# A fused attention and mixture-of-experts kernel: the written-out order of the steps of its middle and last batches is replaced by another

## What is computed

```python
q, k, v = split(x @ W_qkv);  q, k = rope(q, k)
w = softmax(q @ k.T / sqrt(16) + causal_mask)
x = layernorm(x + (w @ v) @ W_o)
gate = top_2(softmax(x @ Wg + bg)), normalized
x = layernorm(x + sum_e gate_e * (x @ We_e.T + be_e))
```

## Time and profile before

| | |
|---|---|
| median of three runs | 3236.32 us (3235.18 to 3238.13) |
| span of the profiled execution | 3236.3 us |
| TensorE (PE) busy | 3109.0 us, 96% |
| VectorE (DVE) busy | 2677.5 us, 83% |
| ScalarE (ACT) busy | 1884.1 us, 58% |
| GpSimd (POOL) busy | 1200.8 us, 37% |
| TensorE clock granted, mean | 0.983 of full speed |

### The profile page before, as it was taken

The page is one execution under the profiler, slowest core; times in us unless marked ns, Lnnn a source line. Parts: engine busy times, 40 slices in busy tenths (PEclk is TensorE's granted clock), DMA queues, the critical chain, the costliest instruction groups (busy, mean ns, idle before and its releaser), DMA issues.

```text
span 3236.3 us, 58547 instructions
## 1 busy us (share of the span) xinstructions
PE 3109.0 (96%) x18752; PEld 1711.5 (53%) x18752; DVE 2677.5 (83%) x8452; ACT 1884.1 (58%) x4253; POOL 1200.8 (37%) x1414
## 2 busy tenths in 40 slices
...
DMA packets 174819, 210.95 MB, mean 65 GB/s; under 512 B 26008, under 2 KB 124592, under 8 KB 174256
## 3 DMA queue, kind: packets, MB, share of 16 engines
q1 hardware_dynamic: 173056, 202.98, 36.1%
...
## 4 chain that ended last, share of the span: by engine, by line
PE 84%; DVE 8%; issue 3%; ACT 2%; DMA 1%; POOL 1%; SPq 0%; ACTq 0%; DVEq 0%; POOLq 0%
PE bank L1052 23%; PE attend L1147 15%; PE scores L1125 14%; PE bank L1109 14%; PE bank L1089 6%; PE bank L1171 3%; PE bank L1098 3%; DVE bank L902 2%; PE bank L1155 1%; PE bank L1077 1%; PE bank L1162 1%; PE bank L1179 1%; DVE maxima L905 1%; PE bank L1203 1%; PE bank L1188 1%
## 5 line engine op out<-in xcount | busy, mean ns | idle before, releaser
L778 ACT ACTIVATE weights<-scores 128x512 f32<-128x512 f32 (+3 forms) x3072 | 1333.1, 494 | 926.0 <-PE scores L1125 913.5
L902 DVE CUSTOM_DVE_ANT_0 bank<-bank,far_q 128x128 f32<-128x128 f32 (+3 forms) x2048 | 962.9, 512 | 202.4 <-PE bank L1109 186.0
L1125 PE MATMUL scores<-q_stack,k_stack 99*128 99x512 bf16 (+3 forms) x3072 | 822.1, 329 | 16.6 <-DMA q_stack<-lowrows 7.3
L1109 PE MATMUL bank<-k_stack,q_stack 96*128 96x512 bf16 (+3 forms) x3072 | 799.5, 332 | 26.3 <-DMA k_stack<-parts_scratch 8.3
L692 POOL TENSOR_SCALAR_AFFINE_SELECT weights<-weights 128x512 f32<-128x512 f32 x512 | 325.5, 637 | 1253.5 <-ACT weights L778 1253.3
L905 DVE TENSOR_REDUCE maxima<-bank 128x1 f32<-128x512 f32 x1024 | 644.1, 682 | 72.6 <-PE bank L1109 72.4
L1147 PE MATMUL attend<-weights,values 128*32 128x512 f32 (+3 forms) x6144 | 583.0, 494 | 1.4 <-POOL weights L692 1.0
L1125 PEld LDWEIGHTS scores<-q_stack,k_stack 99*128 99x128 bf16 x3072 | 279.8, 97 | 417.8 <-ACT weights L778 151.6
L1109 PEld LDWEIGHTS bank<-k_stack,q_stack 96*128 96x128 bf16 x3072 | 276.7, 98 | 398.5 <-issue 166.4
L1052 PE MATMUL bank<-wexp_hi,zT_hi 128*128 128x512 f32 x1024 | 382.2, 454 | 11.1 <-DVE lowrows L922 11.1
L1026 DVE SCALAR_TENSOR_TENSOR z<-bank,picked,z 128x256 f32<-128x256 f32 x512 | 247.6, 484 | 114.6 <-PE bank L1052 105.6
...
## 6 DMA issues: line engine op xcount, KB each, us to landing
parts_scratch<-parts SPq DMA_DIRECT2D x128, 384.0 KB, 2.5
q_stack<-parts_scratch SPq DMA_DIRECT2D x384, 128.0 KB, 7.2
k_stack<-parts_scratch SPq DMA_DIRECT2D x384, 128.0 KB, 7.8
...
q_stack<-lowrows SPq DMA_DIRECT2D x192, 8.0 KB, 2.4
...
```

The costliest lines, as they stand in the source:

```text
L778: act.activation(weights[:, n % NW, hh, c0:CH], st[(QUAD * n + hh) % NS][:, c0:CH], ACT.Exp, scale=DH ** -0.5).then_inc(S["weights_ready"], 1)
L902: dve.tensor_tensor_reduce(out=b[:, 0:w], in0=b[:, 0:w], in1=far_q[:, CH - w:CH], scale=1.0, scalar=-SENTINEL, op0=ALU.add, op1=ALU.max, a ...
L1109: pe.matmul(b[:, 0:w], q_stack[0:ROWS, n, hh, qt * P:(qt + 1) * P], k_stack[0:ROWS, n, hh, kc * CH:kc * CH + w], start=True, stop=True).th ...
L1125: pe.matmul(st[(QUAD * n + hh) % NS][:, c0:CH], k_stack[0:MROWS, s, hh, kb * P:(kb + 1) * P], q_stack[0:MROWS, s, hh, qc * CH + c0:(qc + 1 ...
```

## The change

Two tables of text are replaced, MIDDLE and LAST. Both lists hold the same steps as before, 607 in MIDDLE and 462 in LAST; only their order differs. EARLY, FIRST, POST and all functions stay. LAST is again MIDDLE without the steps that serve a next batch. The core of the diff in MIDDLE (the rows of the table begin with the item of ST that leads them; LAST has the same places):

```diff
-XL.0 XL.1 XT.0 XL.2 XT.1 XL.3 B.0.0.0 B.0.0.1 MC.3
-ST.0.0 ST.0.1 B.0.0.2 B.0.0.3 B.0.1.0 B.0.1.1 ST.0.2 ST.0.3 MASK.0 B.0.1.2 PV.46 PV.47 YE.3.1 B.0.1.3
-ST.1.0 B.0.2.0 ST.1.1 B.0.2.1 ST.1.2 B.0.2.2 ST.1.3 MASK.1
-ST.2.0 MT.3 B.0.2.3 XR.0 XR.1 ST.2.1 YT.3.1 ST.2.2 ST.2.3 MASK.2 PV.0 VCOPY.3 PV.1 XT.2
...
-ST.4.0 B.0.3.2 B.0.3.3 LOAD.0 B.0.4.0 ST.4.1 QK.0.0 ROPE.0.0 B.0.4.1 B.0.4.2 B.0.4.3 ST.4.2 ST.4.3 WO.0.0 PV.2
-  PV.3 YE.0.0
...
-ST.10.0 ST.10.1 GL.0 ST.10.2 N1A.1 ST.10.3 B.0.11.0 MASK.10 B.0.11.1 B.0.11.2 B.0.11.3 PV.8 PV.9 B.1.0.0 YT.0.0
...
-ST.18.0 ST.18.1 B.1.4.3 B.1.5.0 B.1.5.1 B.1.5.2 ST.18.2 ST.18.3 B.1.5.3 PV.16 PV.17 LOAD.1 B.1.6.0 B.1.6.1
...
-ST.23.0 B.1.11.1 ST.23.1 ST.23.2 B.1.11.2 B.1.11.3 B.2.0.0 ST.23.3 MASK.23
...
-ST.37.0 B.3.0.3 B.3.1.0 B.3.1.1 B.3.1.2 ST.37.1 ST.37.2 YT.2.1 MOE.1.2.0 CAST.1.3.1 B.3.1.3 ST.37.3 MASK.37
-  LOAD.3 B.3.2.0
-ST.38.0 ST.38.1 MOE.1.2.1 ST.38.2 ST.38.3 B.3.2.1 B.3.2.2 MT.2 MASK.38 PV.36 PV.37
...
-ST.46.0 N2A.1 ST.46.1 B.3.9.2 VP.1 B.3.9.3 B.3.10.0 B.3.10.1 ST.46.2 ST.46.3 MASK.46 PV.44 PV.45
-ST.47.0 B.3.10.2 B.3.10.3 B.3.11.0 VP.2 B.3.11.1 ST.47.1 B.3.11.2 VP.3 ST.47.2 ST.47.3 MASK.47 B.3.11.3
+B.0.0.0 XL.0
+ST.0.0 ST.0.1 B.0.0.1 ST.0.2 B.0.0.2 PV.46 PV.47 B.0.0.3 B.0.1.0 B.0.1.1 LOAD.0 YE.3.1 MC.3 ST.0.3 B.0.1.2 XT.0
+ST.1.0 B.0.1.3 ST.1.1 B.0.2.0 XL.1 XL.2 ST.1.2 YT.3.1 XT.1 B.0.2.1 MT.3 MASK.0 ST.1.3 B.0.2.2 MASK.1
+ST.2.0 ST.2.1 QK.0.0 ST.2.2 B.0.2.3 B.1.0.0 ROPE.0.0 PV.0 PV.1 B.1.0.1 ST.2.3 B.0.3.0 B.1.0.2 XT.2
...
+ST.14.0 MOE.0.0.1 B.1.5.0 CAST.0.3.1 B.0.10.0 B.0.10.1 ST.14.1 ST.14.2 ST.14.3 MASK.13 PV.12
+ST.15.0 LOAD.1 ST.15.1 MASK.14 MOE.0.0.2 B.0.10.2 ST.15.2 B.0.10.3 ST.15.3 B.1.5.1 PV.13 MASK.15 VCOPY.3 PV.14
...
+ST.19.0 B.2.0.0 B.2.0.1 YT.1.0 ST.19.1 B.1.6.3 B.2.0.2 ST.19.2 QK.1.1 B.1.7.0 B.1.7.1 ST.19.3
...
+ST.23.0 ST.23.1 B.2.2.1 B.2.2.2 ST.23.2 B.2.2.3 ST.23.3 MOE.0.3.1 B.1.9.3 MASK.23 B.2.3.0 MASK.22 CAST.1.1.1
+  B.2.3.1 PV.21 PV.22 PV.23 LOAD.2
...
+ST.29.0 B.3.0.0 B.2.4.3 ST.29.1 QK.1.2 ST.29.2 ST.29.3 GLT.1
...
+ST.42.0 B.3.8.0 YT.2.1 B.2.10.1 ST.42.1 CAST.1.3.0 R2.0 ST.42.2 MOE.1.3.1 B.2.10.2 B.3.8.1 YE.3.0 MOE.1.3.2
+  B.3.8.2 ST.42.3 PV.40 CAST.1.3.1 PV.41 PV.42 LOAD.3 B.3.8.3
+ST.43.0 B.3.9.0 B.3.9.1 ST.43.1 B.3.9.2 B.3.9.3 ST.43.2 ST.43.3 B.2.10.3 B.2.11.0
+ST.44.0 B.2.11.1 MOE.1.3.3 N2A.0 B.2.11.2 ST.44.1 ST.44.2 YT.3.0 N2.1 B.3.10.0 VP.0 B.3.10.1 ST.44.3
+ST.45.0 VP.1 B.3.10.2 ST.45.1 ST.45.2 ST.45.3 MASK.44 R2.1 MASK.45 B.2.11.3 MC.2 N2A.1 PV.43 PV.44 B.3.10.3
+ST.46.0 ST.46.1 ST.46.2 MT.2 VP.2 ST.46.3
+ST.47.0 B.3.11.0 VP.3 B.3.11.1 ST.47.1 B.3.11.2 ST.47.2 ST.47.3 MASK.46 B.3.11.3 MASK.47 PV.45
```

In the old order the B steps of one slot stand together; in the new one those of two slots are mixed for most of the batch. The new LAST starts as follows:

```diff
+B.0.0.0
+ST.0.0 ST.0.1 B.0.0.1 ST.0.2 B.0.0.2 PV.46 PV.47 B.0.0.3 B.0.1.0 B.0.1.1 LOAD.0 YE.3.1 MC.3 ST.0.3 B.0.1.2
+ST.1.0 B.0.1.3 ST.1.1 B.0.2.0 ST.1.2 YT.3.1 B.0.2.1 MT.3 MASK.0 ST.1.3 B.0.2.2 MASK.1
+ST.2.0 ST.2.1 ST.2.2 B.0.2.3 B.1.0.0 PV.0 PV.1 B.1.0.1 ST.2.3 B.0.3.0 B.1.0.2
```

More of the change, by code:

```diff
@@ L204 @@
[L204 to L209, removed]
@@ new lines @@
+ST.1.0 B.0.1.3 ST.1.1 B.0.2.0 XL.1 XL.2 ST.1.2 YT.3.1 XT.1 B.0.2.1 MT.3 MASK.0 ST.1.3 B.0.2.2 MASK.1
+ST.2.0 ST.2.1 QK.0.0 ST.2.2 B.0.2.3 B.1.0.0 ROPE.0.0 PV.0 PV.1 B.1.0.1 ST.2.3 B.0.3.0 B.1.0.2 XT.2
+ST.3.0 B.0.3.1 ST.3.1 MASK.2 B.0.3.2 ST.3.2 XL.3 QK.0.1 B.1.0.3 ST.3.3 XT.3 B.0.3.3 B.0.4.0
+ST.4.0 ST.4.1 B.0.4.1 B.0.4.2 MASK.3 ST.4.2 PV.2 PV.3 CAST.0.0.0 B.0.4.3 HT.0.1 ST.4.3 B.0.5.0 HT.0.0 XR.0
+  B.0.5.1 B.0.5.2
+ST.5.0 YE.0.0 ST.5.1 ROPE.0.1 B.0.5.3 B.1.1.0 B.0.6.0 ST.5.2 ST.5.3 WO.0.0 CAST.0.0.1
@@ new lines @@
+ST.6.0 ST.6.1 B.1.1.1 CAST.0.1.0 WO.0.1 XR.1 HT.1.0 QK.0.2 HT.1.1 B.0.6.1 B.0.6.2 R1.0 B.0.6.3 ST.6.2 ST.6.3
+  N1A.0 YT.0.0 PV.4 PV.5 ROPE.0.2 B.0.7.0
+ST.7.0 ST.7.1 B.0.7.1 B.0.7.2 ST.7.2 B.0.7.3 ZT.0.0 ST.7.3 ZT.0.1 B.1.1.2
+ST.8.0 WO.1.0 ST.8.1 ST.8.2 B.0.8.0 GL.0 CAST.0.1.1 B.1.1.3 B.1.2.0 PV.6 ST.8.3 B.0.8.1 B.1.2.1
+ST.9.0 B.1.2.2 ST.9.1 B.1.2.3 GLT.0 ST.9.2 B.1.3.0 MASK.8 ST.9.3 PV.7 PV.8 MASK.9 GA.0 CAST.0.2.0
+ST.10.0 B.0.8.2 B.0.8.3 GB.0 ST.10.1 ST.10.2 WO.1.1 ST.10.3 B.1.3.1
+ST.11.0 ST.11.1 QK.0.3 ST.11.2 MASK.10 ST.11.3 GT.0 MASK.11 CAST.0.2.1 B.1.3.2 PV.9 PV.10 PV.11 B.0.9.0
@@ new lines @@
+ST.12.0 ST.12.1 B.0.9.1 BE.0.1 ROPE.0.3 B.1.3.3 ST.12.2 ST.12.3 MASK.12 B.0.9.2 BE.0.0 QK.1.0 B.1.4.0
+ST.13.0 ST.13.1 ST.13.2 B.1.4.1 CAST.0.3.0 YE.0.1 B.1.4.2 MOE.0.0.0 B.1.4.3 B.0.9.3 ST.13.3
+ST.14.0 MOE.0.0.1 B.1.5.0 CAST.0.3.1 B.0.10.0 B.0.10.1 ST.14.1 ST.14.2 ST.14.3 MASK.13 PV.12
+ST.15.0 LOAD.1 ST.15.1 MASK.14 MOE.0.0.2 B.0.10.2 ST.15.2 B.0.10.3 ST.15.3 B.1.5.1 PV.13 MASK.15 VCOPY.3 PV.14
+  PV.15 B.0.11.0 ROPE.1.0
+ST.16.0 B.0.11.1 ST.16.1 YT.0.1 ST.16.2 ST.16.3 B.0.11.2 MOE.0.0.3
+ST.17.0 ST.17.1 B.1.5.2 MOE.0.1.0 B.0.11.3 ST.17.2 YE.1.0 MC.0 ST.17.3 R1.1 N1A.1 B.1.5.3 MOE.0.1.1 B.1.6.0
```

163 lines of the change are left out of this document (73 added, 90 removed).

## The result

The changed kernel takes 3473.18 us (3469.85 to 3481.17) against 3236.32 for the kernel before on the same chip: a ratio of 1.0734, 95% interval 1.0718 to 1.0750. One of the four executions of the kernel before, at 3981.93 us, was in a slow state of the chip and is left out. The change makes the kernel slower by 237 us, as forecast (3475, of a range from 3365 to 3575). The profiled execution of after is the slowest of its four, 8 us above the median, with a span of 3479.4 us; that of before had 3236.3.

What follows compares the result with a forecast made beforehand. PE was taken as the bound, newly exposed to transfers on SP's queue. Boundaries 12.5 + 184.6 + 13.0, LOAD.1 and LOAD.2 stalls 35, PV -6: together +239 on 3236.3, so 3475 us, range 3365 to 3575.

Steps and rivals of the forecast that it cites:

- ST.0.0, waiting for MT.2's rows: Batch start: maximum rows, queued behind LOAD.3 and two output stores, land at 187.7 us; ST.0.0 wants them at 184.6.
- from there to XT.1: Batch start: XT.1, due at 188.5 us, waits for XL.1, queued behind LOAD.0 and landing at 202.2; boundary delay 13.7.
- behind XT.1, half clock: After the boundary's long wait PE runs at the 1.2 GHz level; 2.5 us taken, of 0 to 3.2.
- small waits elsewhere: Short PE stalls spread over the batch, left as they were apart from those said to go; 5.0 us.
- LOAD.0's 12 x 1.09 us: SP's queue at the boundary: LOAD.0's twelve transfers take 13.1 us between XL.0 and XL.1.
- the backlog: LOAD.3, two output stores and MT.2 queued on SP ahead of the boundary; delay 13.7 us with them, 12.0 without.
- Into LAST: Boundary into the last batch: B.1.0.0 waits for LOAD.0; 11.2 + 2.5 - 0.7 = 13.0 us.
- The old stalls gone, -1.5 a batch: Batch start: the old stalls at XT.0 and pieces of 0.2 to 0.3 go away, 1.5 us.
- rival B: Faster: LOAD.0 lands within PE's 8.3 us, no boundary stalls, order saves 1.9 a batch; 3208 us, chance 0.04.
- A: SP's queue does not hold XL.1 and MT.2 back, only LOAD.0's own 15.4 us counts; 3370 us, chance 0.13.
- D: The order makes no difference, since SP runs far ahead of PE anyway; 3236 us, chance 0.02.
- C: Clock stays low some 20 us, not 6, after each boundary, +7.5 a boundary; 3587 us, chance 0.09.

Runs made afterwards that it cites:

- old_load_first: The kernel before with only LOAD.0 of the middle batches moved, to between XL.0 and XL.1; 3465.03 us, ratio 1.0705.
- cleared_more: Changed kernel with all XL, XR.0 and XR.1 ahead of LOAD.0, first B.1 later, other loads, casts and stores moved, B steps still mixed; 3257.77 us, ratio 1.0071.
- no_backlog: Changed kernel with R2.0, N2A.0, CAST.1.3 and LOAD.3 earlier and N2A.1 behind MT.2, XL.1 still behind LOAD.0; 3492.38 us, ratio 1.0802.
- old_tweaked: The kernel before with XT.0, XL.2, XT.1, XL.3 behind ST.0.1 and MT.0 ahead of PV.12; 3238.17 us, ratio 1.0007.

## Why the prediction was right

**The bound and the boundary.** Its working says PE is the bound and SP's queue sets when it starts a batch; the timeline, `old_load_first` and `cleared_more` show both. Step by step, with the prediction's numbers for one inner boundary against the mean excess of twelve batches:

| step | predicted, us | measured, us |
|---|---|---|
| ST.0.0, waiting for MT.2's rows | 3.1 | 3.4 |
| from there to XT.1 | 10.6 | 9.1 (6.8 of it the wait) |
| behind XT.1, half clock | 2.5 | 2.5, up to ST.3 |
| B.2.0.0, waiting for LOAD.1 | 0.8 | 0.5 |
| B.3.0.0, waiting for LOAD.2 | 1.7 | 2.2, and 0.6 of half clock behind it |
| small waits elsewhere | 5.0 | 6.0 |
| sum over 184.6 | 23.7 | 24.3 |

**Sizes that were off, and cancel.** LOAD.0's 12 x 1.09 us behind XL.0 were 10.2 in the boundary shown (from 1748.24, where XL.0 landed, to 1758.41) and 11.4 on average, since it moves beside what is queued ahead of it: the first of the twelve landed at 1747.04, ahead of XL.0, and the first window above has 226 GB/s, and no 105. Without the backlog, in `no_backlog`, it was 13.4. So XL.1 came 1.5 us earlier behind ST.0.0 than in the sum, 13.0 for 14.5 on average. PE in turn took some 6.2 us, not 3.9, from ST.0.0 to where it waited for XT.1: the clock fell there too, already behind ST.0.0's wait (0.71 in the second window), which the prediction had not counted. That costs nothing. The two together make XT.1's wait shorter, 6.8 instead of 10.6. `no_backlog` shows the same from the other side: without ST.0.0's wait XT.1 waits 11.4 us on average. The step that was wrong in kind is the backlog: the working gave it 1.7 us a boundary (12.0 without, 13.7 with). It gives nothing; what counts is ST.47.3, and 17 to 19 us from there to XL.1.

**Into LAST** the working had 13.0 us; the wait at ST.0.0 came (4.04 us), but B.1.0.0 waited 1.46 and not some 8.6. Between them PE took 8.1 us for what I had priced at 4.5, at a granted clock of 0.59 (from 3209.7 to 3217.5), and LOAD.0 landed 15.3 us behind ST.47.3 (3203.88 to 3219.2). If LAST's wait at ST.0.0 is counted to the batch that it ends, LAST has 3.0 us for 9.5 predicted (13.0 less 3.1 at ST.0.0 and 0.4 for PV), and the middle batches have 14 more, 1.0 each (measured 209.3, predicted 208.3). The stretch ahead of the middle batches is 3.9 less, in part because two XT now stand behind its last step. That the whole comes within 2 us of the forecast is therefore luck in part: the middle batches are 14 above it, and what stands around them 10 below.

**The old stalls gone, -1.5 a batch**: this step was wrong. `old_tweaked` shows that they move on, and the measured small waits are 6.0, not 5.0. The price of rival B, 3208, counts on it too; `cleared_more`, which has no boundary stall, takes 3258.

**What should show.** The x_in waits once a batch, ST.0.0 on lowrows with 2 to 4.5 us, and the clock are there as described. XT.1's wait is shorter than the 10 us given, the batch 209.3 for 208, and PE's share 92% for 90, because slow matmuls count as busy.

**Rivals.** A is excluded by `old_load_first`, and in after XL.1 landed at 1758.94, behind LOAD.0's last transfer (1758.41); B and D by the time. C, a clock that stays low for some 20 us, isn't seen: 0.50 ends 6.4 us behind XT.1's start.
